# Cross attention's key transfers issued by GpSimd, and last-mixture spreads over 128 rows

## The reference

```python
x = x + L0_xattn(norm(x), ctx, mask)        # 16 heads of 8, masked      -> unit 0
x = x + L0_ffn(norm(x))                     # 8 experts, gelu
x = x + L1_xattn(norm(x), ctx, masks)       # 32 heads of 4, masked      -> units 1 and 2
x = x + L1_ffn(norm(x))                     # top 2 of 8, by capacity
x = x + L2_xattn(norm(x), ctx)              # 16 heads, no mask, alibi   -> unit 3
x = x + L2_ffn(norm(x))                     # quantised product
y = norm(x)
for l in range(4):                          # L3_xattn
    y = y + causal_self_attention(rms(y)) ; y = y + cross(rms(y), ctx, mask)   # -> unit 4+l
    y = y + swiglu(rms(y))
x = x + rms(y)
# last mixture: each token goes to the one expert with the largest probability
probs = softmax(norm(x) @ router_w + router_b); idx = argmax(probs)
x = x + max(probs)[:, None] * (norm(x) @ expert_w[idx] + expert_b[idx])
```

## Time and profile before

| | |
|---|---|
| runs | 2122.28, 2125.67, 2127.61 us; median 2125.67 us |
| the profiled execution's own time | 2126.17 us |
| its span, first to last instruction | 2124.4 us |
| TensorE busy | 1843.6 us, 87% |
| VectorE, ScalarE, GpSimd busy | 1414.4, 1068.8, 663.8 us |
| mean granted TensorE clock | 0.924 of 2.4 GHz |

### The profile page before, as it was taken

How to read it: one execution, slowest core, us unless ns; L and a number is a source line. 1 busy time by engine, 2 the same in 40 slices (tenths; PEclk the granted TensorE clock), 3 DMA queues, 4 the chain that set the end, 5 groups by cost and what they waited for, 6 DMA issues and landing times.

```text
span 2124.4 us, 34572 instructions
## 1 busy us (share of the span) xinstructions
PE 1843.6 (87%) x12971; PEld 1128.1 (53%) x12971; DVE 1414.4 (67%) x3427; ACT 1068.8 (50%) x1523; POOL 663.8 (31%) x903
## 2 busy tenths in 40 slices
PE   5978998684777898899899999999989989989988
PEld 4557664464544454555544564545555554456566
DVE  8667766553776877864677874567785467787474
ACT  2645655131453565564466565366656356656410
POOL 3121112403624453310555320355330245531030
PEclk9979999587787898999999998999999999999987
DMA  7343343121000000141000042000024000013100
GB/s 228 108 126 106 100 112 92 52 82 39 21 1 13 1 1 13 40 115 32 16 1 1 15 106 64 18 1 1 1 71 104 1 16 1 1 29 100 47 1 21
DMA packets 80746, 100.91 MB, mean 47 GB/s; under 512 B 31462, under 2 KB 46190, under 8 KB 79940
## 3 DMA queue, kind: packets, MB, share of 16 engines
q1 hardware_dynamic: 78532, 94.50, 15.7%
q0 software_dynamic: 2048, 4.20, 0.6%
HBM read 52.43 MB, written 12.38 MB: 31 GB/s over the span
## 4 chain that ended last, share of the span: by engine, by line
PE 41%; DVE 13%; ACT 6%; issue 4%; SPq 2%; DMA 2%; POOL 1%; DVEq 0%; POOLq 0%; ACTq 0%
PE wide L841 28%; PE acc L841 13%; DVE maxima L1788 6%; ACT prob L2024 3%; DMA masked_q<-q_g 2%; SPq L765 1%; DVE moments L1324 1%; DVE qkv L1756 1%; ACT prob L1947 1%; DVE hn L1376 1%; DVE hid L1279 1%; SPq L773 1%; ACT hn L1912 1%; DVE hn L1378 0%; ACT q_g L1868 0%
## 5 line engine op out<-in xcount | busy, mean ns | idle before, releaser
L1788 DVE TENSOR_REDUCE maxima<-wide 128x2 f32<-128x512 f32 (+3 forms) x512 | 406.0, 818 | 135.1 <-PE wide L841 131.7
L2024 ACT ACTIVATE prob<-wide 128x768 f32<-128x768 f32 (+1 forms) x384 | 332.3, 881 | 148.8 <-PE wide L841 148.5
L1947 ACT ACTIVATE prob<-wide 77x1024 f32<-77x1024 f32 x256 | 258.1, 1018 | 110.9 <-PE wide L841 109.9
L841 PE MATMUL wide<-q_g 32*128 32x256 f32 (+3 forms) x2048 | 267.6, 393 | 37.0 <-ACT prob L2024 17.9
L2256 POOL TENSOR_SCALAR_AFFINE_SELECT prob<-prob 128x256 f32<-128x256 f32 (+1 forms) x384 | 185.6, 489 | 311.5 <-ACT prob L2024 310.0
L1464 DVE TENSOR_REDUCE maxima<-wide 128x8 f32<-128x616 f32 x256 | 202.9, 795 | 110.5 <-PE wide L841 107.2
L2088 POOL TENSOR_TENSOR rstd<-moments,cst 128x4 f32<-128x4 f32 x88 | 89.8, 1020 | 529.9 <-DVE moments L1352 283.7
L841 PEld LDWEIGHTS wide<-q_g 32*128 32x128 f32 x2048 | 139.4, 187 | 205.3 <-issue 97.6
L1868 ACT ACTIVATE q_g<-wide 128x1024 fp32r<-128x1024 f32 x128 | 131.1, 1025 | 180.7 <-PE wide L841 180.7
L841 PE MATMUL wide<-kx,q_g 128*128 128x312 f32 x512 | 178.1, 413 | 8.3 <-DVE maxima L1464 6.3
L1868 ACT ACTIVATE q_g<-acc 128x512 fp32r<-128x512 f32 x192 | 114.5, 596 | 139.6 <-PE acc L841 134.5
(11 more groups left out here) (247 smaller groups left out, 3007.2 us busy)
## 6 DMA issues: line engine op xcount, KB each, us to landing
masked_q<-q_g SPq DMA_DIRECT2D x448, 64.0 KB
masked_q<-mask_l SPq DMA_DIRECT2D x84, 308.0 KB
masked_k<-kx SPq DMA_DIRECT2D x224, 19.5 KB, 1.8
A<-in_w SPq DMA_DIRECT2D x2, 2048.0 KB, 12.8
unit_w<-in_unit_w SPq DMA_DIRECT2D x8, 448.0 KB, 3.4
ffn_w<-in_ffn_w SPq DMA_DIRECT2D x4, 768.0 KB, 4.7
slots_in<-v_third SPq DMA_DIRECT2D x1, 2560.0 KB, 12.6
prob<-slots_in SPq DMA_DIRECT2D x8, 320.0 KB, 3.2
```

Of the source, the lines that this page charges most:

```text
L841: return e.matmul(out, lhsT, rhs, start=start, stop=stop, is_transpose=turn)
L1788: e.tensor_reduce(top[:, t, h], v[:, :, at0:at0 + P * t + P], AX.X, ALU.max, negate=True).then_inc(*made("max", *([("free", tile)] if t == ...
L1947: e.activation(p[0:SC, :], s[0:SC, :], ACT.Exp, bias=0.0, scale=1.0).then_inc(*made("exp", pb, ("free", tile)))
L2024: e.activation(pv, sv, ACT.Exp, bias=0.0, scale=8 ** -0.5).then_inc(*made("exp", pb, ("free", tile)))
```

## The change

First, `fetch_keys` moves, word for word, from SyncE's program to GpSimd's; its place in ORDER stays. Second, in the last mixture `hot_b` becomes a tile of all 128 rows: GpSimd sets it to zero in a step `m_route` of its own, ScalarE's copy into its first 8 rows waits for that, and `m_spread` contracts over 128 rows (the row of the identity picks the same expert row, the other 120 rows add zeros).

```diff
-            return *four, k[:, 4 * W:4 * W + NI], k[0:E8, S:2 * S], k[0:E8, S // 2:S].bitcast(BF)
+            return *four, k[:, 4 * W:4 * W + NI], k[0:E8, S:2 * S], k[:, S // 2:S].bitcast(BF)
...
         def sync(e):
...
-            def fetch_keys(n, b, half):        # the same function, now in gpsimd(e)
...
         def tensor(e):
...
-                    i_mm = mm(s[:, S * k:S * k + S], ident_b[0:E8, x8:x8 + 1].broadcast_to([E8, P]), hot_t)
+                    i_mm = mm(s[:, S * k:S * k + S], ident_b[:, x8:x8 + 1].broadcast_to([P, P]), hot_t)
...
         def scalar(e):
...
-                for w in need(("m_turn", b)):
+                for w in need(("m_turn", b), ("m_blank", b)):
                     e.wait_ge(*w)
-                copy(hot_b, turned).then_inc(*made("turned", ("m_hot_b", b)))
+                copy(hot_b[0:E8, :], turned).then_inc(*made("turned", ("m_hot_b", b)))
...
         def gpsimd(e):
...
+            def fetch_keys(n, b, half):
+                tile = ("masked_k", n, b, half)
+                at = T.slot("masked_k", tile)
+                for w in need(T.freed("masked_k", tile), ("kv", n, b), ("masked_ones",)):
+                    e.wait_ge(*w)
+                for i in range(HG):
+                    e.dma_start(masked_k[at][0:HR, :, i, :].bitcast(F32),
+                                kx[HR * i:HR * i + HR, i, 2 * half:2 * half + 2, SK * b:SK * b + SK].bitcast(F32)).then_inc(
+                        *landed(f"fetch_keys{at}", *([tile] if i == HG - 1 else [])))
...
+            def m_route(b):
+
+                for w in need(T.freed("prob", ("route", b))):
+                    e.wait_ge(*w)
+                e.memset(moe_views(b)[6], 0.0).then_inc(*made("blank", ("m_blank", b)))
```

More of the change, by code:

```diff
@@ L765, in fetch @@
                     e.dma_start(to[0:HR, ii, :].bitcast(F32), q[r:r + HR, :].bitcast(F32)).then_inc(*landed(sem, *([tile] if ii else [])))
-            def fetch_keys(n, b, half):
[L768 to L775, removed]
             def extras():
@@ L821, in m_store @@
                     *landed(f"out{b}", ("stored", b)))
-            do = dict(mask_turn=mask_turn, fetch=fetch, fetch_keys=fetch_keys, unit_end=unit_end, f0_down=f0_down, f0_hidden=f0_hidden, mask_load=mask_load, extras=extras, masks3=masks3, slots_in=slots_in_,
+            do = dict(mask_turn=mask_turn, fetch=fetch, unit_end=unit_end, f0_down=f0_down, f0_hidden=f0_hidden, mask_load=mask_load, extras=extras, masks3=masks3, slots_in=slots_in_,
                       f1_out=f1_out,
@@ L2270, in gpsimd @@
                       q_cut=q_cut, out_project=out_project, add_o=add_o, f0_next=f0_next, clear=clear,
-                      scatter=scatter, gather=gather, bias_u=bias_u,
+                      scatter=scatter, gather=gather, m_route=m_route, fetch_keys=fetch_keys, bias_u=bias_u,
                       f2_matmul=f2_matmul, masks3=masks3, cut_q=cut_q, cut_k=cut_k, self_logits=self_logits,
```

## The result

The changed kernel has a median of 2113.92 us over 21 runs (2103.94 to 2128.8), the kernel before 2127.32 us over 21 runs (2113.24 to 2146.77). The ratio is 0.9937, with a 95% interval from 0.9919 to 0.9955: 13.4 us less, between 9.6 and 17.2. The predicted median was 2114 us. One pair of profiles therefore shows a larger difference (18.1 us of span) than the kernels have.

A forecast was written before the change was run, and what follows sets the result against it. TensorE, busy 87% of the span, was taken as the bound, so only its waits and half-clock time count. Terms -10.0 - 4.0 + 0.5 + 3.0 + 2.2 - 3.5 = -11.8 us gave 2114 us, range 2099 to 2135 (8 in 10).

The forecast's parts named there:

- SyncE's side, the stalls: Tails of five units: without the key block ahead, the first mask is issued 1.9 us earlier; 2.0 us each, -10.0 us.
- Rival B: Tails limited by landing and slots, not issue: 3 us of the 10 remain, none of the clock; 2127 us, chance 0.20.
- The clock of the tails: Tails of units 4 to 6: a third of the 12.2 us they take beyond unit 7's, -4.0 us.
- Rival A: Clock and stalls both come back in full, -33 us at best; half of the extra gives 2102 us; chance 0.12.
- The argument against more: Tails of units 4 to 6: ScalarE is busy some 10 us in each, so TensorE stays loosely fed; only a third taken.
- GpSimd's side: Key transfers issued by GpSimd: 1.26 us each, 5.1 us per block of four, delaying some of its other operations.
- three terms: GpSimd's delays: power -1/2 for batch 3 in four units +0.5, start of unit 0 +3.0, routing of unit 2 +2.2 us.
- The start of unit 0: First key block from 34.5 to 39.6 makes `q_project` 2.1 us late, and the power follows late; +3.0 us in all.
- the causal masks of unit 4: Last self-attention item: masks 2.5 us late behind a key block, but covered, so nothing taken; without cover +10 over units 4 to 7.
- The fit ahead of `q_project`: Batches 2 and 3 of a unit: a 5.1 us block fits by 0.1 us; cover gone from 1.30 us per transfer.
- The last mixture: Spreads over 128 rows bring the clock back earlier: one group of expert multiplications in each of two batches, -3.5 us.
- Rival D: The clock of the last mixture doesn't answer to height: 2117 us; counted inside the forecast's own chance of 0.49.

The follow-up runs named there:

- split4: The changed kernel with each key transfer on GpSimd split in four of 8 rows (896 transfers); ratio to the kernel before 1.0727, 2290.49 us.
- tail_keys: The kernel before with only the 56 key transfers of each masked unit's last batch moved to GpSimd, mixture as before; ratio 0.9966, 7.2 us less.
- sp_earlier: The kernel before with the first half of the next batch's keys one pair earlier in ORDER, still on SyncE; ratio 0.9927, 15.5 us less.
- best: The kernel before with keys one pair earlier on SyncE and spreads over 128 rows; ratios 0.9891 and 0.9907 in two measurements, 2110.28 and 2108.64 us.
- height_only: The kernel before with only the spreads over 128 rows, keys still on SyncE; ratio 0.9981, 4.0 us less, and 0.9971 when run again.
- split2: The changed kernel with each key transfer on GpSimd split in two of 16 rows (448 transfers); ratio to the kernel before 0.9924.

## Why the prediction was right

**SyncE's side, the stalls: right in place and size.** The forecast took 10.0 us of the 16.1 away. The total of the waits for masked_q is 16.1, 16.8 and 15.9 us in the three kernels with the old order, and 4.1, 6.1, 7.9, 4.6, 6.6 and 4.4 us, 5.6 on average, in the six with all keys on GpSimd and blocks of up to 4 us (all but split4): 10.7 us. In the tails of units 4 to 7 alone they are 8.8, 9.1 and 8.3 us with the old order, 0.7 to 2.4 in the six, and 2.1 to 2.8 with the keys a pair earlier on SyncE. tail_keys and sp_earlier show that the place of the block ahead of the tail's first mask is the cause. Rival B, by which the mask's landing and not its issue would be late, is out: it left only 3 us of gain there.

**The clock of the tails: right in direction, a little small.** The forecast took 4.0 us. The four tails take 66.0 us on average with the old order (67.0, 70.8, 60.2) and 60.0 on average in the same six kernels: 6.0 us. Rival A's mechanism, a return to full clock with ScalarE as busy as before, is what the windows show, in three tails of four; only sp_earlier and the two versions of best come near its price of 12.2 us (55.3 on average, 10.7 less). That price was read from one trace by taking unit 7 as the tail that runs well; in height_only, with the same order, unit 7's tail takes 17.5 us, so it was no different from the others. The argument against more, that TensorE would stay loosely fed, was weak: it is busy 11.7 to 12.0 us of the 14 us of a tail, and is granted full clock all the same. Without the stall the clock still falls in one tail of three, and why in these is not shown.

**GpSimd's side: the step that was mis-sized.** 5.7 us were counted, in three terms, all from a block of 5.1 us. A block is 2.2 us, 0.54 us per transfer. The lower bound too, SyncE's own 0.607, was above it: what an indirect transfer costs GpSimd is no guide to a plain one. (The landing time of 2.8 us was the shortest of the earlier trace rows, whose median is 3.2; nothing hangs on it.) One reading behind a term was wrong as well. The start of unit 0 was dated by SyncE's first key transfer, at 34.5; that was when SyncE came to it, not when the keys were there. GpSimd's timeline in the changed kernel:

```profile
28.16 2.34 POOL L2163 DMA_DIRECT2D masked_k<-kx  x4
37.91 1.03 POOL L2095 TENSOR_TENSOR qkv<-qkv,alive 128x512 f32<-128x512 f32 x1 [7.41 <-DVE qkv L1420]
...
40.95 2.15 POOL L2163 DMA_DIRECT2D masked_k<-kx  x4
45.25 1.04 POOL L2078 TENSOR_TENSOR rstd<-moments,cst 128x4 f32<-128x4 f32 x1 [2.15 <-DVE moments L1345]
```

The block was out before `q_project` was wanted, and 7.41 us of idle time stay ahead of it; it and the power start 0.4 us later than before, not 2 to 3, and with idle time ahead of them that VectorE ends, so the block isn't what delays them. At the routing of unit 2, the same timeline:

```profile
321.77 2.15 POOL L2163 DMA_DIRECT2D masked_k<-kx  x4
...
326.54 1.04 POOL L2078 TENSOR_TENSOR rstd<-moments,cst 128x4 f32<-128x4 f32 x1 [1.63 <-issue]
```

This power has 1.63 us of idle time ahead of it still. So the term is near 0, not +5.7. That the causal masks of unit 4 would come 2.5 us late fell with it. The fit ahead of `q_project` was right: 5.2 us by the prediction, 4.99 by split2.

The Trainium skill, "SBUF — State Buffer", section "A bandwidth-pool intuition that's wrong (but worth ruling out)", has a transfer issued from GpSimd take about 3100 ns beside a copy on VectorE where it takes about 620 ns alone. No run here tests that case: the trace has the landing of 112 of the 224 transfers, and VectorE ran no copy and no cast between the start and the landing of any of them; beside 107 it ran a reduce. Beside the work that VectorE does here the price doesn't arise: the transfers took 533 to 735 ns of GpSimd, and the longest of the 112 landed after 4.0 us.

**The last mixture: right, a little small.** The forecast took 3.5 us for a clock that comes back earlier. With spreads over 8 rows the stretch is 80.1, 85.5, 79.2, 82.2, 86.2 and 78.5 us long, 82.0 on average; with 128 rows it is 76.4, 76.3, 74.9, 75.6, 76.0, 77.9 and 75.1, 76.0 on average. No value of one group lies in the other, and the difference is 5.9 us. Rival D, that the clock doesn't answer to the height, is out. The spreads themselves cost the same, as forecast: 376/379/634 ns (shortest, median, longest) over 128 rows in the changed kernel, 374/438/629 over 8 in the kernel before. The shortest are those at full clock, the longest those at half clock, and the median follows how many ran at which.

**The sum.** -10.7 - 6.0 - 5.9 = -22.6 us, against -13.4 measured and -11.8 forecast. But these terms may not be added: 1.9 us of the waits with the old order, and 0.6 in the six, stand inside the windows of the tails and count twice, and a wait that ends isn't all won. Laid end to end the traces give less. From the start to the mixture the three kernels with the old order take 2042.7 us on average and the six 2030.7, 12.0 us less. Of these, 6.6 went between the first and the second pair of the tails of units 4 to 7, 6.0 in the windows behind, and 2.2 in the tail of unit 0; the rest of the program took another 0.7. Against them stand 3.5 us given back: from the feed-forward block of units 4, 5 and 6 to the first product of the next tail the old order takes 959.5 us, with 22.8 at half clock, and the six take 963.0, with 33.6. The six values run from 959.7 to 967.1 and the old ones from 957.8 to 961.1, so this is a tendency, and what brings these falls of the clock about is not shown.

With the mixture's 5.9 us that makes 17.9 us. The two parts measured alone, 9.2 and 16.4, and 4.0 and 6.2, add to the same on average. The changed kernel's own ratio gives 13.4 and allows 17.2. From the start to the mixture single profiles under one order differ by 10 to 13 us, so 4.5 us can be scatter; where they go otherwise is open. So the closeness of the forecast, 2114 against 2113.9, is luck in part. Its gains, 17.5 us, are near the 17.9, but its cost of 5.7 us isn't there, and happens to stand where the measured time falls short of the parts.

## What to carry to other kernels

A hand-written queue is read at the places where its neighbours' slots come free: a block of transfers that stands just ahead of one whose slot is already free delays that one and all behind it, and moving the block one step forward on the same queue can give as much as moving it to another engine. A stall of 2 us at the edge of a stage can cost more than itself, since the clock can fall behind it (here in 12 tails of 12, and in 9 of 36 without it); look at PEclk of the stretch that follows. Before work goes to a less busy engine, work out how long a block fits ahead of its next obligation: doubled it cost nothing here, and doubled again it cost 170 us.

## What the runs showed of the hardware

In the last mixture, multiplications over few rows go with a lower granted clock. The same stretch, with the same instructions on TensorE and nearly the same time for a spread at full clock (374 and 376 ns), had 32.7 to 50.2 us at half clock with 32 spreads over 8 rows (six profiles), 36.3 over 32 rows (one), and 18.4 to 32.0 over 128 rows of which 120 held zeros (seven).

GpSimd issues a plain transfer of 19.5 KB in 0.536 us and one of half or a quarter of its rows in 0.504 and 0.560 us (the medians of split2 and split4): here the cost hardly depends on the bytes. The 112 transfers whose landing the trace has land after 1.9 us (median), SyncE's after 1.8. An indirect one took 0.960 us of GpSimd.
